# Gate logits and ranks of the second pass on four 128x32 column tiles each

## The chip, the cores and the metric

One core of a Trainium2 chip runs one program. The metric is the device time of one execution in microseconds (us); the median of three runs stands for a kernel. TensorE works on stationary weights (loaded by a weight load, LDWEIGHTS) and moving columns (MATMUL); an fp32 product is recorded as two pairs of load and matmul, a transpose as one pair.

## The reference

128 sequences of 32 tokens with 512 channels (4096 tokens) pass three residual layers: cross attention to a context, a gated delta-rule attention, and a mixture of eight experts of which each token takes two. What matters here is the end of the second layer and the third:

```python
ctx = _rmsnorm(ys, norm_w) * jax.nn.silu(gate)
x = x + (ctx.reshape(b, l, D_OUT) @ Wo.T + bo)
...
logits = xf @ gate_w.T                 # xf = layernorm(x), 4096 x 512; gate_w 8 x 512
w, sel = jax.lax.top_k(logits, TOP_K)  # two experts a token, softmax over the two
...
out = jnp.einsum('ne,ned->nd', w_full, expert_out)
```

## The kernel before

The tokens are cut into 32 units of 128 (NU = 32). A first pass computes cross attention, the projections and the delta rule and leaves its results in device memory; its loops are not touched. The second pass, which the function second_pass writes out without loops, has four parts:

- a stretch of turns w = 0 to 26 (BEFORE = 27), one after the other;
- the tiles of the first part of the tokens (24 units), each 128 rows for one expert (turn_tile, mix_tile);
- the remaining turns, w = 27 to 34, cut in three thirds each and placed between tiles 32 to 49 of that list (function inserted);
- the tiles of the second part, while GpSimd gathers the two results of each token and VectorE adds them up (combine).

A turn w is a pipeline stage that serves several units at once. TensorE does, in this order: (third 0) transposes the normalised rows x2n of unit w-3 into turn_bank, computes y of unit w+1 as 64 products of 32x32 tiles (make_y), transposes context of unit w-1; (third 1) the logits of unit w-3 from x2n_t and gate, then the output product wo of unit w-1; (third 2) the ranks of unit w-3, which count how many earlier tokens chose each expert. The logits have the stationary operand x2n_t (four chunks of 128x128) and eight moving columns; the ranks have two stationary 128x128 matrices (earlier, ones) and eight moving columns. Both go through the helper products at L118 to L121, as does wo, so that all three carry line L120 in the profile; they are told apart by the names of their tiles (small_bank<-gate,x2n_t; small_bank<-member,earlier; small_bank<-taken,ones; wo_bank<-wo,context_t).

Between the two transposes ScalarE copies turn_bank out (move_x2n L1410, move_context L1404): the logits wait for the first copy, wo for the second. VectorE takes the logits in choose (L1503 to L1518), which ends with the tile taken; the ranks wait for that (member_ready). VectorE then uses the ranks in place (L1527), which gives each token its row for the scatter that GpSimd issues. A turn's x2n for the next transposes comes from VectorE as well (scaled, L1497). Each engine runs its own list in order and waits on semaphores. SyncE issues the loads and stores of each unit, the experts' weights (1 MB each, in every second turn at first) and the tiles' rows.

Of the kernel before, what the change touches and what calls it, by code (L numbers as in the profile page):

```python
# [12 lines left out]
B, N, D = 128, 32, 512  # L13
M, C = 257, 384
H, HD = 16, 32
E = 8
P = 128
BU = P // N
NU = B // BU
DC, CC = D // P, C // P  # L20
# [97 lines left out]
def products(pe, out, terms, start=True, stop=True):  # L118
    for i, (lhs_t, rhs) in enumerate(terms):
        last = pe.matmul(out, lhs_t, rhs, start=start and i == 0, stop=stop and i == len(terms) - 1)  # L120
    return last  # L121
# [971 lines left out]
def second_pass(nc, ident, early, rows, wo_t, bo, gate_t, expert_t, out):  # L1093
    with ExitStack() as ctx:
        def sb(name, shape, dt=F32):
            return ctx.enter_context(nc.sbuf_tensor(name, shape, dt))

        def sem(name):
            return ctx.enter_context(nc.semaphore(name))
# [6 lines left out]
        gate = sb("gate", [P, DC, E])  # L1106
        bo_s = sb("bo_s", [P, D])
        earlier = sb("earlier", [P, P])
        ones = sb("ones", [P, P])
# [19 lines left out]
        x2n_t = sb("x2n_t", [P, DC, P])  # L1129
# [12 lines left out]
        member = sb("member", [P, 2, E])  # L1142
        taken = sb("taken", [P, 2, E])
# [23 lines left out]
        small_bank = ctx.enter_context(nc.psum_tensor("small_bank", [P, D], F32))  # L1167
# [17 lines left out]
        member_ready, ranks_ready, ranks_read = sem("member_ready"), sem("ranks_ready"), sem("ranks_read")  # L1185
# [24 lines left out]
        def inserted(t):  # L1210

            n, places = 3 * (NU + 3 - BEFORE), INSERT_END - INSERT_AT
            return [(BEFORE + i // 3, i % 3) for i in range(n) if INSERT_AT + i * places // n == t]
# [383 lines left out]
        @block.tensor  # L1597
        def _(pe):
            def make_y(w):
                g, q = w // GU, w % GU  # L1600
                if q == 0 or w == 0:
                    pe.wait_ge(group_loaded[g % 2], (g // 2) * 320 + 320)
                if w > 1:
                    pe.wait_ge(y_read, w - 1)
                for h in range(H):
                    for b in range(BU):
                        seq, at, head = slice(N * q, N * q + N), slice(N * b, N * b + N), slice(HD * h, HD * h + HD)
                        last = pe.matmul(y[at, w % 2, head], qk[g % 2][seq, b, head], delta[g % 2][seq, b, head],  # L1608
                                         start=True, stop=True)
                last.then_inc(y_ready, 1)  # L1610

            def turn_rows(to, row, done):
                for c in range(DC):
                    last = pe.transpose(to[:, c, :], row[:, c * P:c * P + P], ident[:])  # L1614
                last.then_inc(done, 1)

            def turn(w, third):
                if third == 0:
                    if w >= 3:
                        pe.wait_ge(x2n_ready, w - 2)  # L1620
                        pe.wait_ge(context_moved, min(w - 1, NU))
                        turn_rows(turn_bank, x2n[:, (w - 3) % 2], x2n_turned)
                    if w + 1 < NU:
                        make_y(w + 1)
                    if 0 <= w - 1 < NU:
                        pe.wait_ge(context_ready, w)
                        if w > 2:
                            pe.wait_ge(x2n_moved, w - 2)
                        turn_rows(turn_bank, context[:, (w - 1) % 2], context_turned)
                if third == 1:  # L1630
                    if w >= 3:
                        pe.wait_ge(x2n_moved, w - 2)
                        if w > 3:
                            pe.wait_ge(ranks_read, w - 3)
                        products(pe, small_bank[:, 0:E], [(x2n_t[:, c, :], gate[:, c, :]) for c in range(DC)])\
                            .then_inc(logits_ready, 1)
                    if 0 <= w - 1 < NU:
                        pe.wait_ge(context_moved, w)
                        if w > 1:
                            pe.wait_ge(x2_ready, w - 1)  # L1640
                        products(pe, wo_bank[:], [(context_t[:, c, :], wo[:, c, :]) for c in range(DC)])\
                            .then_inc(wo_ready, 1)
                if third == 2 and w >= 3:
                    r = w - 3
                    pe.wait_ge(member_ready, r + 1)
                    products(pe, small_bank[:, E:2 * E],
                             [(earlier[:], member[:, r % 2]), (ones[:], taken[:, r % 2])]).then_inc(ranks_ready, 1)
                    if r + 1 in (FIRST[1], NU):
                        pe.matmul(small_bank[:, 2 * E:3 * E], ones[:], taken[:, (r + 1) % 2], start=True, stop=True)\
                            .then_inc(totals_ready, 1)  # L1650

            def turn_tile(t):
                pe.wait_ge(xs_loaded[t % 4], 16 * (t // 4) + 16)
                if t > 0:
                    pe.wait_ge(xs_moved, t)
                turn_rows(xs_bank, xs[:, t % 4], xs_turned)

            def mix_tile(t, expert):
                pe.wait_ge(xs_moved, t + 1)
                if t >= 2:  # L1660
                    pe.wait_ge(y_moved, t - 1)
                products(pe, mix[t % 2][:], [(xs_t[:, t % 2, c, :], experts[:, bass.ds(expert + c * D, D)])
                                             for c in range(DC)]).then_inc(mixed, 1)

            def expert_of(t):
                part = int(t >= START[1])
                if t in START:
                    pe.wait_ge(lists_ready, part + 1)
                return pe.value_load(expert_at[0:1, part, t - START[part]:t - START[part] + 1], min_val=0,
                                     max_val=(E - 1) * DC * D)  # L1670

            make_y(0)
            for w in range(BEFORE):
                for third in range(3):
                    if (w, third) == (1, 1):
                        pe.wait_ge(outputs_loaded, 32)
                    if (w, third) == (3, 2):
                        pe.wait_ge(constants, 1)
                    turn(w, third)
            pe.wait_ge(experts_loaded, 16 * E)  # L1680
            expert = expert_of(0)
            turn_tile(0)
            for t in range(sum(TILES)):
                if t + 1 < sum(TILES):
                    following = expert_of(t + 1)
                    turn_tile(t + 1)
                mix_tile(t, expert)
                expert = following
                for w, third in inserted(t):
                    turn(w, third)  # L1690
# [43 lines left out]
```

## Time and profile before

| | |
|---|---|
| median of three runs | 3275.37 us (3274.96 to 3275.93) |
| span of the profiled execution | 3280.0 us |
| first pass, to about | 2590 us |
| turns w = 3 to 26 | 2622.82 to 2847.65 us |
| turns between tiles | 2990 to 3125 us |

The profiled execution's own time is its span, from the first to the last instruction; no further time of it is given, and it lies 4.6 us above the median. In the profile, PE is TensorE's matmul side and PEld its weight loads. A timeline line gives the start in us, the duration, the engine, the kernel's line, the operation, output<-inputs, the shape of the tile (rows*columns of the array, then the moving operand), how many instructions are merged, and in brackets the idle time ahead and what ended it ("issue": nothing that the profile shows).

### The profile page before, as it was taken

What the parts mean: (1) busy time and instruction counts of PE and PEld (TensorE: products, weight loads), DVE (VectorE), ACT (ScalarE), POOL (GpSimd) and SP (SyncE); (2) the same over time, 40 slices, a digit from 0 to 9 for tenths busy, and PEclk for the clock granted to TensorE, in tenths of its full rate; (3) what the DMA queues carried; (4) which work ended last, traced back from release to release, by engine and by line L of the source; (5) the groups of instructions that cost most, each with busy time, mean ns of one, the idle gap of its engine ahead of it and who ended that gap; (6) DMA issues with size and microseconds to landing.
All of it is one profiled execution on the core that took longest, in us unless ns stands there. A gap on an engine that the chain in (4) does not pass through costs nothing. (4 is left out here: it accounts for less than half of the span.)

```text
span 3280.0 us, 87701 instructions
## 1 busy us (share of the span) xinstructions
PE 3097.4 (94%) x35570; PEld 2267.9 (69%) x35570; DVE 2009.3 (61%) x4107; ACT 1337.9 (41%) x3360; POOL 641.3 (20%) x514
## 2 busy tenths in 40 slices
PE   7999999999999999999999999999999788898984
PEld 5777777777777777777777777777777455544542
DVE  3333367666776677666667766667676477893323
ACT  3444444444444444444444444444443233322321
POOL 0011111111111111111111111111111376601234
PEclk9999999999999999999999999999999888899997
DMA  4222322232222222322232223222321688545479
GB/s 168 69 73 76 105 93 91 86 103 84 81 79 98 85 81 85 98 84 81 79 102 90 81 79 102 84 81 86 108 82 55 170 255 247 166 135 157 145 264 324
DMA packets 297853, 378.10 MB, mean 115 GB/s; under 512 B 159568, under 2 KB 211536, under 8 KB 296016
## 3 DMA queue, kind: packets, MB, share of 16 engines
q1 hardware_dynamic: 287184, 338.19, 32.7%
q0 software_dynamic: 10240, 33.56, 3.0%
q8 instruction: 346, 5.67, 0.7%
q14 instruction: 83, 0.68, 0.1%
HBM read 258.17 MB, written 189.01 MB: 136 GB/s over the span
## 5 line engine op out<-in xcount | busy, mean ns | idle before, releaser
L120 PE MATMUL ring<-cond_high,wkv_high 128*128 128x342 f32 (+1 forms) x1152 | 404.6, 351 | 43.7 <-issue 20.8
L120 PE MATMUL ring<-cond_low,wkv_high 128*128 128x342 f32 (+1 forms) x1152 | 371.4, 322 | 0.0
L120 PE MATMUL ring<-cond_high,wkv_low 128*128 128x342 f32 (+1 forms) x1152 | 370.3, 321 | 0.0
L615 ACT ACTIVATE shared_rows<-ring,kvb 128x342 f32<-128x342 f32 (+1 forms) x384 | 209.6, 546 | 376.6 <-PE ring L120 376.6
L840 DVE TENSOR_REDUCE neg_max<-score 128x4 f32<-128x1028 f32 x128 | 157.3, 1229 | 288.3 <-PE score L952 288.3
L120 PE MATMUL ring<-wkv_high,cond_high 128*128 128x512 f32 x768 | 316.6, 412 | 0.0
L169 DVE TENSOR_TENSOR prod<-coef,deltas 128x64 f32<-128x64 f32 (+30 forms) x248 | 306.8, 1237 | 5.9
L120 PE MATMUL ring<-wkv_high,cond_low 128*128 128x512 f32 x768 | 303.1, 395 | 0.0
L120 PE MATMUL ring<-wkv_low,cond_high 128*128 128x512 f32 x768 | 302.7, 394 | 0.0
L649 ACT ACTIVATE prob<-score,neg_max 128x257 f32<-128x257 f32 x512 | 236.5, 475 | 135.3 <-DVE neg_max L840 135.3
L120 PE MATMUL mix<-experts,xs_t 128*128 x624 | 287.1, 604 | 0.0
L120 PEld LDWEIGHTS ring<-cond_high,wkv_high 128*128 128x128 f32 x1152 | 219.0, 190 | 92.9 <-issue 54.2
L173 DVE TENSOR_TENSOR prod<-prod 128x256 f32<-128x256 f32 (+5 forms) x352 | 258.1, 733 | 12.1
L569 POOL TENSOR_TENSOR vgb<-vgb,steps_of 128x512 f32<-128x512 f32 x32 | 40.5, 1265 | 1067.2 <-ACT steps_of L644 1067.2
L120 PE MATMUL ring<-wattn,x1n_t 128*128 128x512 f32 x512 | 246.7, 615 | 0.3 <-ACT prob L622 0.3
L120 PE MATMUL ring<-x1n_t,wattn 128*128 128x128 f32 x2048 | 238.9, 278 | 0.0
L120 PEld LDWEIGHTS ring<-x1n_t,wattn 128*128 128x128 f32 x2048 | 233.7, 194 | 0.0
L120 PEld LDWEIGHTS ring<-cond_low,wkv_high 128*128 128x128 f32 x1152 | 218.6, 190 | 15.1 <-issue 15.1
L610 ACT ACTIVATE v_s<-ring 128x512 f32<-128x512 f32 x256 | 154.4, 603 | 157.8 <-PE ring L120 157.8
L120 PEld LDWEIGHTS ring<-cond_high,wkv_low 128*128 128x128 f32 x1152 | 218.7, 190 | 0.0
L120 PEld LDWEIGHTS mix<-experts,xs_t 128*128 128x128 f32 x624 | 115.3, 195 | 116.5 <-issue 116.5
L120 PEld LDWEIGHTS ring<-wkv_high,cond_high 128*128 128x128 f32 x768 | 144.4, 188 | 63.1 <-issue 34.8
(199 smaller groups left out, 5499.8 us busy)
## 6 DMA issues: line engine op xcount, KB each, us to landing
cond<-cond_t_dram SPq DMA_DIRECT2D x128, 385.5 KB, 4.2
xs<-slot_rows SPq DMA_DIRECT2D x78, 256.0 KB, 2.8
slot_rows<-ys SPq DMA_DIRECT2D x78, 256.0 KB, 2.0
x_rows<-x SPq DMA_DIRECT2D x64, 256.0 KB, 2.7
vb_rows<-vgb SPq DMA_DIRECT2D x64, 256.0 KB, 3.4
x_in<-x_dram SPq DMA_DIRECT2D x32, 256.0 KB, 3.4
kk_rows<-kk_rows_s SPq DMA_DIRECT2D x32, 256.0 KB, 2.7
qk_rows<-decay SPq DMA_DIRECT2D x32, 256.0 KB, 2.8
```

What stands on the lines that cost most here:

```text
L120: last = pe.matmul(out, lhs_t, rhs, start=start and i == 0, stop=stop and i == len(terms) - 1)
L169: own.then(dve.tensor_tensor(tiles["prod"][:, 0:t], coef, tiles["deltas"][:, 0:t], ALU.mult))
L173: own.then(dve.tensor_tensor(tiles["prod"][:, 0:half], tiles["prod"][:, 0:half], tiles["prod"][:, left:whole], ALU.add))
L569: own.then(pool.tensor_tensor(vgb[:, 1], vgb[:, 1], steps_of[:].rearrange("p h t -> p (h t)"), ALU.mult))
L610: act.activation(dst, ring_bank[bank][:], func, **how).then_inc(ring.free[bank], 1)
L615: act.activation(k_t[:, group, at:at + n], ring_bank[bank][:, 0:n], ACT.Identity, bias=kvb[:, group:group + 1]).then_inc(ring.free[bank], 1)
L649: act.activation(prob[:, b % 2, g, :], score[:, g, 0:M], ACT.Exp, bias=neg_max[:, g:g + 1], accum_out=sums[:, g:g + 1]).then_inc(exp_done, 1)
L840: dve.tensor_reduce(neg_max[:], score[:, :, 0:M], AX.X, ALU.max, negate=True)\
```

## The change

The products of the logits and of the ranks no longer go through products but through a new by_quarter, which cuts the stationary operand into four blocks of 32 columns. Each block gives 32 of the 128 output partitions, in its own 128x32 column tile of the array. One product becomes four. The operands, the waits, the semaphores and the order of the work stay as they are; the single product for the totals stays whole.

```diff
+            def by_quarter(out, terms):
+                for i, (lhs_t, rhs) in enumerate(terms):
+                    for at in range(0, P, N):
+                        last = pe.matmul(out[at:at + N, :], lhs_t[:, at:at + N], rhs, start=(i == 0),
+                                         stop=(i == len(terms) - 1))
+                return last
+
...
-                        products(pe, small_bank[:, 0:E], [(x2n_t[:, c, :], gate[:, c, :]) for c in range(DC)])\
+                        by_quarter(small_bank[:, 0:E], [(x2n_t[:, c, :], gate[:, c, :]) for c in range(DC)])\
                             .then_inc(logits_ready, 1)
...
-                    products(pe, small_bank[:, E:2 * E],
-                             [(earlier[:], member[:, r % 2]), (ones[:], taken[:, r % 2])]).then_inc(ranks_ready, 1)
+                    by_quarter(small_bank[:, E:2 * E],
+                               [(earlier[:], member[:, r % 2]), (ones[:], taken[:, r % 2])]).then_inc(ranks_ready, 1)
```

N is 32, P is 128.

## Rows read from the trace of the kernel before

**Rows 1.** The page's first line.
```profile
span 3280.0 us, 87701 instructions
```

**Rows 2.** Windows: stretch and its us, busy us (instructions) by engine, PEclk, DMA share, GB/s.
```profile
2622.82:2847.65 224.83, 200.41 (x3746) 132.00 (x3746) 177.59 (x573) 80.58 (x168) 159.55 (x118) 0.86 0.81 233
...
2990.00:3125.00 135.00, 126.05 (x964) 71.50 (x965) 44.78 (x180) 46.88 (x92) 35.91 (x30) 0.96 0.45 150
```

**Rows 3.** Windows of two turns, and of 20 turns in a row.
```profile
2707.39:2714.42 7.03, 7.03 (x159) 4.91 (x158) 6.27 (x25) 3.31 (x7) 4.50 (x3) 1.00 0.45 121
...
2722.29:2730.87 8.58, 7.72 (x156) 5.05 (x156) 7.88 (x25) 3.44 (x8) 6.74 (x6) 1.00 1.12 318
2629.87:2820.13 190.26, 167.25 (x3122) 110.15 (x3122) 148.14 (x482) 67.01 (x140) 133.02 (x98) 0.86 0.87 248
```

**Rows 4.** Timeline of TensorE's matmuls in the shortest of these turns.
```profile
2707.96 1.29 PE L1608 MATMUL y<-delta,qk 32*32 32x32 f32 x128
2709.17 0.66 PE L1614 MATMUL turn_bank<-ident,context 128*128 128x128 f32 x4
2709.66 0.96 PE L120 MATMUL small_bank<-gate,x2n_t 128*128 128x8 f32 x8
2710.52 3.70 PE L120 MATMUL wo_bank<-wo,context_t 128*128 128x512 f32 x8
2714.05 0.28 PE L120 MATMUL small_bank<-member,earlier 128*128 128x8 f32 x2
...
2714.42 0.63 PE L1614 MATMUL turn_bank<-ident,x2n 128*128 128x128 f32 x4
```

**Rows 5.** The same view at the ranks two turns later.
```profile
2729.99 0.39 PE L120 MATMUL small_bank<-member,earlier 128*128 128x8 f32 x2 [0.51 <-DVE taken L1518]
```

**Rows 6.** Windows of six turns: two of them, and the sum line of all six.
```profile
2645.35:2656.97 11.62, 10.00 (x156) 6.52 (x157) 8.62 (x26) 4.87 (x11) 9.44 (x8) 0.71 1.09 299
...
2682.32:2691.53 9.21, 9.12 (x157) 5.68 (x157) 8.52 (x26) 4.33 (x9) 7.27 (x6) 0.81 0.95 263
...
sum 79.35, PE 61.31 PEld 39.29 DVE 49.39 ACT 22.74 POOL 50.54; mean PE 10.22 PEld 6.55 DVE 8.23 ACT 3.79 POOL 8.42
```

**Rows 7.** Timeline of TensorE's matmuls in three of these turns.
```profile
2645.93 1.67 PE L1608 MATMUL y<-delta,qk 32*32 32x32 f32 x128
...
2649.86 1.45 PE L120 MATMUL small_bank<-gate,x2n_t 128*128 128x8 f32 x6 [1.54 <-issue]
...
2657.53 1.09 PE L1608 MATMUL y<-shared_rows 32*32 32x32 f32 x104
2660.17 0.39 PE L1608 MATMUL y<-shared_rows 32*32 32x32 f32 x24 [1.55 <-issue]
...
2697.98 0.44 PE L1608 MATMUL y<-delta,qk 32*32 32x32 f32 x16 [4.73 <-issue]
```

**Rows 8.** DMA view, 2622 to 2848: queue, packets, MB, share of 16 engines.
```profile
q8 instruction: 29, 0.48, 0.9%
```

**Rows 9.** Timeline of TensorE's matmuls in the first pass, around a column-tiled group.
```profile
1503.76 0.39 PE L120 MATMUL ring<-wkv_low,cond_high 128*128 128x512 f32 x1
1503.99 0.40 PE L120 MATMUL ring<-wkv_high,cond_low 128*128 128x512 f32 x1
1504.31 0.76 PE L982 MATMUL ring<-prob_t,v_s 128*32 128x32 f32 x64
1505.01 0.42 PE L986 MATMUL ring<-prob_last_t,v_last_s 4*32 4x128 f32 x8
```

**Rows 10.** Timeline of all engines in the turn of rows 4.
```profile
2709.86 0.60 ACT L1404 ACTIVATE context_t<-turn_bank 128x512 f32<-128x512 f32 x1 [1.21 <-PE turn_bank L1614]
...
2710.51 0.30 PEld L120 LDWEIGHTS wo_bank<-wo,context_t 128*128 128x128 f32 x2
```

**Rows 11.** Timeline of TensorE's matmuls between tiles.
```profile
3038.70 0.95 PE L120 MATMUL small_bank<-gate,x2n_t 128*128 128x8 f32 x8
3039.51 3.68 PE L120 MATMUL wo_bank<-wo,context_t 128*128 128x512 f32 x8
```

## The prediction

> **What bounds the kernel now.** I read the page first: the profiled execution spans 3280.0 us [rows 1], 4.6 us over the median of the timed runs (3275.37). I make the sum against the span and carry the difference over to the median unchanged. The changed lines run only in the second pass, so I split that pass by windows [rows 2]. Two stretches hold them: 2622.82 to 2847.65 (stage A: 24 turns of the second pass back to back, w = 3 to 26, 224.83 us, granted clock 0.86 on the mean, DMA share 0.81) and 2990 to 3125 (stage B: the last 8 turns between expert tiles, TensorE busy 126.05 of 135 us). Whatever stage A gains or loses moves all that follows, since the expert tiles start only after the last ranks of stage A.
>
> In stage A the reader is to look at single turns. The shortest takes 7.03 us [rows 3], and in it TensorE has no gap [rows 4]: y, the turned context, logits (2709.66 to 2710.52, 0.86 us), wo (3.53 us), ranks (0.37 us), the turned x2n. The turn but one after it takes 8.58 us at the full clock [rows 3], and ends in a wait of TensorE, 0.51 us, for VectorE's taken [rows 5]. So TensorE and VectorE are almost equally long per turn. But the mean of 20 turns is 190.26 / 20 = 9.5 us [rows 3]: 49.7 us above 20 x 7.03. Most of that lies in six turns, together 79.35 us, or 37.2 above 6 x 7.03 [rows 6]. Each holds a gap of TensorE marked "issue" (three of them in [rows 7]): between two matmuls of one group, with no semaphore in between. After such a gap the granted clock is at its lower level (1.2 GHz) for part of the turn (on the mean 0.81 even in the cheapest of the six [rows 6]).
>
> **What these gaps are.** Count the matmuls from the gap at 2649.86 to the gap at 2660.17: 6 logits, 8 wo, 4 ranks, 4 turns of x2n, 104 of y [rows 4, 7] make 126. Each has its weight load: 252 instructions, with three or four waits 256. The DMA view gives 29 instruction packets of 16 KB for stage A [rows 8], and 2 x 3746 matmuls and loads [rows 2] with four waits a turn, over 256, are 29.6. So TensorE takes its instructions in blocks of 256 by DMA, and a gap is a block that came late, with the data queues at 0.81 of the DMA engines. In the turn from 2645.35 two block ends lie close together, one 14 instructions into y, which starts at 2645.93, the other after two of the eight logits matmuls [rows 7]: the next block was there only at 2649.86, 3.9 us after the first end.
>
> The Trainium skill, Runtime: NRT & Kernel Launch, section Instruction fetch mechanics, also has 16 KiB blocks of 256 instructions, fetched while the current one runs, but holds the cost of a block's end to be mostly hidden. The gaps of stage A speak against the second half; by the rule the sum would be that of rival 1.
>
> **The change part by part.** *Logits.* Eight pairs of load and matmul become 32, each load of 32 columns. The trace has this form in the first pass: 64 pairs of 128x32 tiles from 1504.31 to 1505.01, 0.70 us or 11 ns a pair [rows 9]; the 128 pairs of y take 1.21 us or 9.5 ns [rows 4]. So 32 pairs take 0.30 to 0.35 us. Going into the tiled form costs 0.09 us: the 512-column matmul before it holds TensorE 0.32 us (1503.99 to 1504.31) where the one ahead of it held TensorE 0.23 us (1503.76 to 1503.99). Coming back, wo's first load can no longer run ahead; no row isolates that, so between nothing and two pairs of loads (2 x 0.107 us, from 0.86 / 8); I take one. Together 0.09 + 0.35 + 0.11 = 0.55 us (0.39 to 0.65) against 0.86: 0.3 us less.
>
> *Is that on the path?* In stage A, no: ScalarE copies the turned context from 2709.86 to 2710.46, and wo's first load goes at 2710.51 [rows 10]. It waits for that copy, which the logits just cover; shorter logits leave TensorE idle in its place. Uncovered, 0.3 us a turn would be 7 us. Where the clock is low the logits outlast the copy, so I credit 0.3 us in stalled turns. In stage B, six turns of eight have a tile between the turned context and the logits, so the copy is long done and wo follows at once (3038.70 to 3039.51 [rows 11]): 6 x 0.27 = 1.6 us less.
>
> *Ranks.* Four pairs in 0.37 us become 16: 0.09 + 16 x 0.011 + 0.11 = 0.38 us. Nothing, within 0.1 us either way (8 turns of B: 0.8 us at most; in A taken by the slack towards VectorE).
>
> *Instructions.* Logits +48, ranks +24: a turn grows from 312 and four waits (316) to 388. Blocks per turn go from 1.23 to 1.52; two turns are 776 = 3 x 256 + 8, so block ends recur at the same places every second turn, 8 earlier each time. Where? Before, a turn moves them 60 earlier. From instruction 270 of the fourth turn (the gap at 2649.86) back over three turns: 194 into the y of the first turn, and nothing ahead of it changes. From there on, at 388 a turn: ends at 62 and 318 in the second turn, 54 and 310 in the fourth, down to 6 and 262 in the sixteenth, -2 and 254, -10 and 246 after that. y covers 0 to 255, the logits 268 to 332. So in some ten turns a whole block lies in y and logits, which TensorE eats in some 1.2 + 0.5 + 0.2 = 1.9 us; the trace showed 3.9 us for its delivery. Before, such a pair of ends came about every fifth turn.
>
> The sum over the same 20 turns. Of the ten stalled ones I price each as the turn from 2645.35, whose block ends lie alike: 11.62 us [rows 6], 4.6 over 7.03. Of the other 20 blocks I let three be late by chance, as two of about 20 were before, at the mean of six turns, 37.2 / 6 = 6.2 us. That is 46 + 18.6 = 64.6; less 0.3 x 13 = 4 for the logits; plus 3 for VectorE's waits in the seven quiet turns (up to 1.55 us a turn before, as 8.58 shows; less now, since each stall lets VectorE catch up). 63.6 against 49.7: **14 us more**. Bounds: at the cheapest stall (9.21 - 7.03 = 2.2 us [rows 6]) it is 39.6, 10 us less than before; at 6.2 us each it is 80, 30 more. I take the middle one because its geometry is the new one. Stage B: -1.6, and 1 for one late block in its eight turns. Sum +13.4: span 3293, median **3289 us**.
>
> **The rivals.** *1. Blocks arrive in time or their lateness is lost in VectorE's lag.* Then stage B's 1.6 us and some 0.4 us in six half-clock turns are all: -4, **3271**. For it: after 2813 the gaps are gone, and longer turns thin out the DMA traffic. Against: 3.9 us for a block that is eaten in 1.9. It decides once a block is there in 2 us.
>
> *2. Faster: the logits are on the path.* If wo could start when they end, 24 x 0.3 + 1.6 = 9 us go: **3266**. For it: TensorE has no gap in the shortest turn. Against: wo's load at 2710.51, 0.05 us behind the copy's end. It decides where ScalarE's copy ends before the logits do. The Trainium skill, TensorEngine Tiling (Array Packing), section Theoretical Speedup, allows up to 4x for 32-wide tiles; by that the logits would take an estimated 0.21 us, and 0.65 x 24 + 3.6 make 19 us.
>
> *3. The changes of form cost more than 0.09 us.* Four a turn stand where none stood. From 0.25 us each at both ends the logits gain nothing (0.25 + 0.35 + 0.25) and the ranks lose 0.3 us in each of 32 turns (0.25 + 0.18 + 0.25 against 0.37): 10 us, **3285** without any late block. Against: the two rows that show such a change.
>
> **How the numbers follow.** Forecast 0.62, rival 1 0.17, rival 2 0.11, rival 3 0.10. A measurement of this kernel tells 0.2% (6.5 us) from no change. The forecast's own range is 3277 to 3306 and gives 0.56 to slower and 0.06 to same; rival 1 gives 0.14 to same and 0.03 to faster; rival 2 0.11 to faster; rival 3 0.08 to slower and 0.02 to same. Faster 0.14, same 0.22, slower 0.64. The range is 3269 to 3306: below lies rival 2 and the tail of rival 1, above a mean stall beyond 6.2 us.
>
> **What would show it.** Right: logits at 0.5 us in quiet turns while wo still starts 0.05 us behind ScalarE's copy; 35 to 37 instruction packets in stage A; "issue" gaps in y, the turned context or the logits of every second turn from the second on; a lower mean clock in stage A; logits and wo 0.3 us closer in stage B. Wrong: gaps as many as before or all under 1 us; wo following the logits directly; or logits still at 0.8 us.

## The result and the profile after

The changed kernel takes 3288.85 us against 3277.6 us (medians of 20 runs each, side by side on one chip), a ratio of 1.0031 with an interval of 1.002 to 1.0042: slower by 0.31%, some 10 us. The forecast was 3289 us and slower. The runs of one kernel scatter more than the first three showed (3271.66 to 3291.59 before, 3278.96 to 3301.98 after), and single profiles scatter likewise, which the readings below have to bear. The profiled execution took 3290.16 us; its page begins

```profile
span 3288.1 us, 90005 instructions
```

Its span is 8.1 us above that of before [rows 1]. Windows of the kernel after (stretch and its us, busy us and instructions by engine, granted clock, DMA share, GB/s), as in [rows 2, 3]:

```profile
2622.70:2853.90 231.20, 188.27 (x4609) 108.43 (x4610) 175.32 (x573) 80.26 (x168) 157.46 (x116) 0.86 0.76 225
...
2629.74:2828.70 198.96, 159.34 (x3847) 91.42 (x3841) 147.91 (x482) 66.95 (x140) 133.56 (x98) 0.85 0.81 238
2702.34:2709.36 7.02, 6.70 (x202) 4.02 (x193) 6.27 (x25) 3.31 (x7) 4.50 (x3) 1.00 0.46 125
2709.36:2722.78 13.42, 9.13 (x202) 5.05 (x193) 9.47 (x25) 3.42 (x7) 8.96 (x7) 0.75 0.88 274
```

The reader is to see three things. Stage A takes 231.2 us, 6.6 more than between the same two instructions before (224.6, to 2847.4), and the 20 turns of [rows 3] take 198.96 instead of 190.26: 8.7 more, of which the other four turns, one ahead of them and three behind, give 2.1 back (32.2 us, before 34.3). A quiet turn is as long as ever, 7.02 us, although TensorE is now busy for only 6.70 of it. And every second turn looks like the last line: 13.42 us, at a granted clock of 0.75. In it TensorE stands still for 4.29 us in the logits, and wo behind them runs at the lower clock: 5.87 us, where a quiet turn's wo takes 3.70.

```profile
2716.73 5.87 PE L120 MATMUL wo_bank<-wo,context_t 128*128 128x512 f32 x8
```

The DMA view of stage A, queue of the instructions, as in [rows 8]: 36 packets where 29 were, 0.59 MB, which is 16.4 KB each.

```profile
q8 instruction: 36, 0.59, 1.1%
```

The timeline of TensorE's matmuls, the counterpart of [rows 7]: the first seven of the stage's 11 gaps over 1 us (five were there before), and one in the turned context and one in y, from later turns. After "x" stands how many matmuls of the group were still to come.

```profile
2635.12 0.24 PE L1620 MATMUL small_bank<-gate,x2n_t 128*32 128x8 f32 x6 [2.57 <-issue]
...
2652.86 0.38 PE L1620 MATMUL small_bank<-gate,x2n_t 128*32 128x8 f32 x10 [2.23 <-issue]
...
2673.93 0.40 PE L1620 MATMUL small_bank<-gate,x2n_t 128*32 128x8 f32 x15 [5.14 <-issue]
...
2695.92 0.50 PE L1620 MATMUL small_bank<-gate,x2n_t 128*32 128x8 f32 x19 [5.15 <-issue]
...
2716.29 0.51 PE L1620 MATMUL small_bank<-gate,x2n_t 128*32 128x8 f32 x23 [4.29 <-issue]
...
2735.19 0.60 PE L1620 MATMUL small_bank<-gate,x2n_t 128*32 128x8 f32 x27 [2.78 <-issue]
...
2756.45 0.62 PE L1620 MATMUL small_bank<-gate,x2n_t 128*32 128x8 f32 x32 [4.47 <-issue]
...
2776.90 0.90 PE L1614 MATMUL turn_bank<-ident,context 128*128 128x128 f32 x3 [4.36 <-issue]
...
2795.28 0.25 PE L1608 MATMUL y<-delta,qk 32*32 32x32 f32 x3 [2.05 <-issue]
```

The gaps move forward by four or five pairs from one to the next, that is by 8 to 10 instructions every second turn, through the logits, then the turned context, then y: a period of 256 instructions against two turns of 776. All 11 lie in every second turn.

The trace's list of DMA packets has the blocks themselves. Ahead of each of the 11 gaps' ends a 16 KB packet of the instruction queue moves for 0.89 to 1.22 us and lands 1.30 to 1.54 us before the matmuls go on; ahead of the five gaps of before it lands 1.26 to 1.47 us before. In the five gaps of over 4 us the packet starts to move only 1.9 to 2.9 us after the gap has begun. So a gap is a late block, and what is late is the start of its transfer.

All engines in the quiet turn, as in [rows 4, 10]:

```profile
2704.14 0.66 PE L1614 MATMUL turn_bank<-ident,context 128*128 128x128 f32 x4
...
2704.73 0.44 PE L1620 MATMUL small_bank<-gate,x2n_t 128*32 128x8 f32 x32
2704.84 0.60 ACT L1404 ACTIVATE context_t<-turn_bank 128x512 f32<-128x512 f32 x1 [1.21 <-PE turn_bank L1614]
...
2705.49 0.30 PEld L120 LDWEIGHTS wo_bank<-wo,context_t 128*128 128x128 f32 x2 [0.41 <-ACT context_t L1404]
```

The logits take 0.44 us instead of 0.96 by this view. The load for wo comes at 2705.49, 0.05 us behind the end of ScalarE's copy (2704.84 + 0.60), as before; what the logits saved has become a wait of 0.41 us.

Stage B, from the x2n transposes of w = 27 to the last ranks, by windows. Before:

```profile
3001.84:3114.50 112.66, 109.83 (x919) 63.19 (x918) 41.28 (x163) 42.60 (x85) 33.99 (x28) 1.00 0.42 144
```

After:

```profile
3009.84:3124.84 115.00, 108.33 (x1207) 56.15 (x1205) 41.29 (x163) 42.56 (x85) 33.98 (x28) 1.00 0.42 141
```

TensorE is busy 1.5 us less and the stage is 2.34 us longer; 0.6 less was forecast. The timeline of TensorE's matmuls after shows where; its logits are to be set beside those of [rows 11]:

```profile
3032.13 0.44 PE L1620 MATMUL small_bank<-gate,x2n_t 128*32 128x8 f32 x32
3032.49 3.70 PE L120 MATMUL wo_bank<-wo,context_t 128*128 128x512 f32 x8
3036.12 0.25 PE L1620 MATMUL small_bank<-member,earlier 128*32 128x8 f32 x8
3036.21 0.23 PE L1620 MATMUL small_bank<-taken,ones 128*32 128x8 f32 x8
...
3036.90 0.63 PE L1614 MATMUL xs_bank<-ident,xs 128*128 128x128 f32 x4 [0.46 <-issue]
```

And before, the same ranks and the tile's transposes behind them:

```profile
3027.69 0.28 PE L120 MATMUL small_bank<-member,earlier 128*128 128x8 f32 x2
3027.83 0.37 PE L120 MATMUL small_bank<-taken,ones 128*128 128x8 f32 x2
3028.06 0.63 PE L1614 MATMUL xs_bank<-ident,xs 128*128 128x128 f32 x4
```

From the logits to wo 0.36 us pass where 0.81 did. But from the ranks to the next tile 0.78 us pass (3036.12 to 3036.90) where 0.37 did, and 0.46 of them are "issue". Six of the eight rank groups are followed by a tile and take 0.77 to 0.82 us; the two that are followed by x2n transposes take 0.24, less than before. In the last two turns a tile follows the logits, and there 0.86 and 1.12 us pass up to it, so that the logits gain 1.6 us over the stage (6.56 to 4.97) and not 8 x 0.45.

### The profile page after: what moved, and what is told of

Read it like the earlier page. It is cut to its first block and busy times, and to the rows that moved or that the text cites. A ratio compares the mean times of both kernels' runs of the same rounds, so it can differ in the third digit from the quotient of the medians.

```text
span 3288.1 us, 90005 instructions
## 1 busy us (share of the span) xinstructions
PE 3081.9 (94%) x36722; PEld 2235.9 (68%) x36722; DVE 2008.4 (61%) x4107; ACT 1337.4 (41%) x3360; POOL 638.5 (19%) x514
## 5 line engine op out<-in xcount | busy, mean ns | idle before, releaser
L120 PE MATMUL ring<-wattn,x1n_t 128*128 128x512 f32 x512 | 246.7, 615 | 0.3 <-ACT prob L622 0.3
```

## The experiments

All kernels of one group of chip runs were timed beside the kernel before on the same chip; that kernel's medians were 3274.71, 3282.53 and 3282.85 us in the three groups (3277.6 beside the kernel after), so only ratios are compared. "Per turn" counts TensorE's instructions in a turn of stage A with its four waits. Stage times are those of one profile each.

| kernel | per turn | ratio of times | stage A, us | stage B, us |
|---|---|---|---|---|
| before | 316 | | 224.6 | 112.7 |
| after | 388 | 1.0031 [1.002, 1.0042] | 231.2 | 115.0 |
| logits alone | 364 | 1.0011 [0.9998, 1.0024] | 223.7 | 112.4 |
| ranks alone | 340 | 0.999 [0.9975, 1.0004] | 223.3 | 115.8 |
| y repeats, no tiles | 388 | 1.0088 [1.0066, 1.0109] | 246.7 | |
| one y repeat, no tiles | 320 | 0.9983 [0.9972, 0.9995] | 222.7 | 112.5 |
| block ends in wo | 384 | 1.0014 [0.9998, 1.0029] | 229.9 | 111.4 |
| block ends in logits | 384 | 1.0048 [1.0029, 1.0067] | 247.5 | |
| tiles late | 320 | 1.0005 [0.9987, 1.0023] | 214.8 | 118.4 |
| experts' loads first | 388 | one run | 224.8 | |
| expert read early | 388 | 1.001 [0.9995, 1.0026] | 227.1 | 109.0 |
| logits late | 320 | 0.9972 [0.9953, 0.999] | 216.2 | 111.3 |
| tiles late, read early | 320 | 0.9985 [0.997, 0.9999] | 214.9 | 110.5 |

### Each half alone

Logits on column tiles, ranks as before:

```diff
-                    by_quarter(small_bank[:, E:2 * E],
-                               [(earlier[:], member[:, r % 2]), (ones[:], taken[:, r % 2])]).then_inc(ranks_ready, 1)
+                    products(pe, small_bank[:, E:2 * E],
+                             [(earlier[:], member[:, r % 2]), (ones[:], taken[:, r % 2])]).then_inc(ranks_ready, 1)
```

> The logits on column tiles, the ranks whole. Theory (late instruction blocks): a turn has 364 instructions instead of 316, block ends move 108 a turn, and a whole block lies in y, turned context and logits (or from the ranks to the next y) in about 8 of 24 turns, against 5 before and 11 after: 5 us over before (0 to 9), some 8 instruction gaps of over 1 us in stage A. Rival A (the change of form is what costs): two changes of form a turn instead of four, 5 us over before too, but with as few gaps as before. Rival B (the logits' saving reaches the path): faster than before.

Measured: 1.0011, not to be told from no change, with ten gaps over 1 us in stage A (27.3 us together, 15.8 before) but a stage no longer than before. So more gaps do not by themselves make a longer stage: before, turns without a gap take up to 8.58 us [rows 3] with TensorE waiting for VectorE, and behind a stalled turn such waits are missing (7.02 us after). In stage B the logits fall to 5.00 us in all (6.56 before) and the ranks stay at 3.13.

Ranks on column tiles, logits as before:

```diff
-                        by_quarter(small_bank[:, 0:E], [(x2n_t[:, c, :], gate[:, c, :]) for c in range(DC)])\
+                        products(pe, small_bank[:, 0:E], [(x2n_t[:, c, :], gate[:, c, :]) for c in range(DC)])\
```

> The ranks on column tiles, the logits whole. Theory: 340 instructions a turn, block ends move 84 a turn, a short block every third turn, of which only some four end before wo: 1 us over before (-3 to 4), 4 to 6 gaps of over 1 us. Rival A: 5 us over before, as with the logits alone.

Measured: 0.999, five gaps, stage B 115.8 us. The ranks take 5.19 us in stage B instead of 3.13, with the whole logits beside them: the loss of stage B is theirs alone, and it is there with or without the tiled logits.

### Instructions without tiles

The same number of instructions as after, by computing some y products twice in the turns of stage A, in the kernel before:

```diff
-                for h in range(H):
-                    for b in range(BU):
...
+                pairs = [(h, b) for h in range(H) for b in range(BU)]
+                more = 18 if 3 < w <= BEFORE else 0
+                for h, b in pairs + pairs[len(pairs) - more:]:
...
```

> The kernel before, with no new column tile: 18 of y's 64 products of each unit from the turn w = 3 on are computed a second time, with the same operands into the same place. That adds 72 instructions a turn, as many as the change, in the form that y has anyway. Theory: 388 instructions a turn, so block ends stand as after the change and TensorE waits in every second turn; 11 us as after, plus 0.3 us for the repeats in the quiet turns: 14 us over before (8 to 20), some 11 gaps. Rival A: no new change of form, so only the repeats' 0.3 us in the turns that TensorE sets: 2 to 4 us over before, with five or six gaps.

Measured: 1.0088, 29 us, with gaps in every second turn again, nine of them over 1 us. The timeline of TensorE's matmuls of this kernel:

```profile
2630.54 0.32 PE L1609 MATMUL y<-delta,qk 32*32 32x32 f32 x5 [2.53 <-issue]
...
2653.88 0.36 PE L1609 MATMUL y<-delta,qk 32*32 32x32 f32 x9 [5.53 <-issue]
...
2677.05 0.43 PE L1609 MATMUL y<-shared_rows 32*32 32x32 f32 x14 [5.10 <-issue]
```

Column tiles are not needed for the gaps: 72 more cheap instructions a turn make them by themselves, and again the gap moves by four or five pairs each time. The size was missed by half, the loss being twice the 14 us forecast. Part of it is the repeats' own time: a quiet turn takes 7.35 us instead of 7.02, some 8 us over 24 turns of the 22 that stage A is longer than before. The gaps over 1 us are not longer (32.0 us together, 37.6 after), but stalled turns take 10 to 16 us here. One reason that fits is that these gaps lie in y, ahead of the turned context and so ahead of ScalarE's copy, where those of the change mostly lie in the logits, beside it; that is argued and no run separates it.

One repeated product a turn (and six once), so that the turn has 320 instructions, 5/4 of a block:

```diff
+                more = 1 if 3 < w <= BEFORE else 6 if w == 3 else 0
```

> The kernel before, with one of y's products repeated in each turn from w = 3 on (4 instructions, 320 a turn) and six repeated once in the turn ahead (24 instructions). Four turns are then five blocks exactly, and the one turn in four that has two block ends has the second in the middle of wo, so that no block is eaten in under 3.8 us. Theory: gaps are left only where a block waits over 2 us longer than usual behind data: 2 to 4 of them, 5 us under before (-12 to 0). Rivals: 20 to 40 ns a turn more, no difference that can be measured, five or six gaps.

Measured: 0.9983, about 5.6 us faster with work added, nearly what was expected. But five gaps exceed 1 us (1.06 to 3.55), so the block ends were not all freed; the time came as expected, its picture only in part.

### Where the block ends lie

Two kernels with tiled logits, whole ranks and five repeats a turn (384 instructions, 3/2 of a block, so that ends stay where they are put): the first with 22 repeats once at the start, which puts one of the three block ends of two turns into wo and the others into y, the second with 5, which leaves one in the logits.

```diff
+                more = 5 if 3 < w <= BEFORE else 22 if w == 3 else 0
```

> The logits on column tiles, the ranks whole, five of y's products repeated in each turn from w = 3 on: 384 instructions a turn, so two turns are three blocks and the block ends stay where they are. 22 products repeated once in the turn ahead put the ends at about 102 and 230 of y and in the middle of wo. Theory: no block is eaten in under 3.6 us, so only a block that waits long behind data comes late: 3 to 5 gaps of over 1 us, and the time at or below that of before (-8 to +2). Rival A (the forms cost): within 3 us of the next kernel.

```diff
+                more = 5 if 3 < w <= BEFORE else 5 if w == 3 else 0
```

> The same kernel with 5 instead of 22 products repeated once: 68 instructions less in the whole program, 384 a turn as well. The ends now lie at about 42 and 170 of y and in the logits, so that in every second turn a block is eaten in about 1.7 us. Theory: 11 or 12 gaps in stage A, 12 to 25 us over the kernel with the ends in wo, although it does 0.3 us less work. Rival A: no difference, or 0.3 us faster.

Measured: 1.0014 and 1.0048. The second is some 10 us slower with 68 instructions fewer, so where the ends lie costs time by itself. But the first missed its expectation: eight gaps over 1 us remain in its matmuls (ten in its weight loads), where 3 to 5 were expected; the second has fourteen. Weight loads in its timeline:

```profile
2639.40 0.44 PEld L1609 LDWEIGHTS y<-delta,qk 32*32 32x32 f32 x21 [3.28 <-issue]
...
2654.62 0.19 PEld L120 LDWEIGHTS wo_bank<-wo,context_t 128*128 128x128 f32 x1 [1.46 <-issue]
...
2662.85 0.50 PEld L1609 LDWEIGHTS y<-delta,qk 32*32 32x32 f32 x21 [4.94 <-issue]
```

The block that came at 2654.62, with wo's last three matmuls, was eaten by 2657.91 (2662.85 - 4.94). That is 3.3 us instead of the 1.9 that the prediction set against a delivery of 3.9, and the next one still came 4.94 us late, 8.2 us after the block ahead of it. So in stage A not even a block of 3.3 us is safe. The timeline of TensorE's matmuls in the second kernel:

```profile
2652.63 0.51 PE L1621 MATMUL small_bank<-gate,x2n_t 128*32 128x8 f32 x24 [4.19 <-issue]
...
2673.92 0.51 PE L1621 MATMUL small_bank<-gate,x2n_t 128*32 128x8 f32 x25 [5.17 <-issue]
```

The gap in the logits stays at one place, as 3/2 of a block a turn says, and comes in every second turn.

### What makes a block late

The kernel after, with the experts' 8 MB loaded ahead of the second pass's first turn instead of between turns; DMA share in stage A falls from 0.76 to 0.70.

```diff
+            for e in range(E):
+                sp.dma_start(experts[:, e * DC * D:(e + 1) * DC * D].rearrange("p (c n) -> p c n", c=DC),
+                             expert_t[e].rearrange("(c p) n -> p c n", p=P)).then_inc(experts_loaded, 16)
             for w in range(BEFORE):
                 follow(w)
...
-                if w % 2 == 1 and w < 2 * E:
-                    e = w // 2
-                    sp.dma_start(experts[:, e * DC * D:(e + 1) * DC * D].rearrange("p (c n) -> p c n", c=DC),
-                                 expert_t[e].rearrange("(c p) n -> p c n", p=P)).then_inc(experts_loaded, 16)
```

> The changed kernel, with the loads of the experts' weights (8 x 1 MB) issued in one go ahead of turn 0 instead of one in every second turn up to w = 15. That leaves the instructions of TensorE as they are and takes 8 MB out of the queues during stage A. Theory: the gaps stay in every second turn at the same instructions, but those up to w = 16, 2.4 to 5.3 us in the changed kernel, shrink to 1.3 to 2.5 us, since a block no longer waits behind an expert; stage A gets shorter by 10 us or more, while the turns ahead of it start later. If the gaps were a cost of the forms, they would keep their lengths.

The timeline of its TensorE matmuls:

```profile
2655.66 0.29 PE L1619 MATMUL small_bank<-gate,x2n_t 128*32 128x8 f32 x6 [1.83 <-issue]
...
2673.26 0.38 PE L1619 MATMUL small_bank<-gate,x2n_t 128*32 128x8 f32 x10 [2.21 <-issue]
...
2691.97 0.31 PE L1619 MATMUL small_bank<-gate,x2n_t 128*32 128x8 f32 x15 [1.89 <-issue]
...
2709.49 0.36 PE L1619 MATMUL small_bank<-gate,x2n_t 128*32 128x8 f32 x19 [2.01 <-issue]
```

The same instructions as after (x6, x10, x15, x19) and shorter gaps: the first seven are 1.83, 2.21, 1.89, 2.01, 1.35, 2.98 and 1.21 us, 13.5 in all, where the kernel after has 26.6 and the kernel with the expert read early, whose stage A is the same, 22.3. In six of the seven the block's packet already moves when the gap begins. Stage A is 6.4 us shorter, less than the 10 or more expected, and no more than single profiles of one and the same stage A differ by (214.8 to 222.7 us with one repeat a turn). The whole kernel is not better (3301.74 us in its one timed run), because the loads hold up the start of stage A by 18 us (2640.92 instead of 2622.70). So the gaps depend on the traffic of the data queues, and some 2 us of each remain without the experts' loads.

### The tiles only where the path has use for them

Tiles in stage B alone (turns from w = 27 on), stage A with one repeat a turn as above; against the kernel after, cut:

```diff
-                        by_quarter(small_bank[:, 0:E], ...
+                        (by_quarter if w >= BEFORE else products)(pe, small_bank[:, 0:E], ...
-                    by_quarter(small_bank[:, E:2 * E], ...
+                    (by_quarter if w >= BEFORE else products)(pe, small_bank[:, E:2 * E], ...
```

> The column tiles only in the last eight turns, between the expert tiles, where wo follows the logits at once; in stage A both products whole, with one repeated product of y a turn (and six once) as in the kernel with 320 instructions a turn. Theory: 5 us under before as that kernel, and 0.35 us less in each of the six late turns that show the logits on the path, 2 us: 7 us under before (-13 to -2). If tiles cost in the late turns, it is no faster than the kernel with 320 instructions.

A miss: 1.0005. Stage A is short, 214.8 us, but stage B takes 118.4, even longer than after, with 5.24 us in the ranks. This, and the 0.46 us of "issue" after the ranks, brought up the suspicion that the next step tests. Ahead of each tile TensorE's program reads the tile's expert number into a register (expert_of). It may be that this read can't run ahead of 32 short rank instructions and stands in the open.

The kernel after, with that read moved ahead of the turn's inserted thirds:

```diff
             turn_tile(0)
+            following = expert_of(1)
             for t in range(sum(TILES)):
                 if t + 1 < sum(TILES):
-                    following = expert_of(t + 1)
                     turn_tile(t + 1)
                 mix_tile(t, expert)
                 expert = following
+                if t + 2 < sum(TILES):
+                    following = expert_of(t + 2)
                 for w, third in inserted(t):
                     turn(w, third)
```

> The changed kernel, in which TensorE reads the number of each tile's expert into a register (expert_of) one tile earlier: ahead of the inserted thirds of a turn instead of behind them. Theory: in the changed kernel the ranks' and logits' 96 instructions keep TensorE's sequencer from running ahead to that read, which costs 0.4 to 0.5 us behind the ranks in six of the last eight turns (0.77 to 0.82 us from ranks to the next tile, against 0.36 before). With the read ahead of them, behind a tile's 3.4 us, the ranks take 0.24 us in all eight turns and the stretch of these turns gets from 115.0 to 111 or 112 us (112.65 before); the total time 3 us under the changed kernel, still over before for stage A. Rival: the 0.4 us is a cost of going back from column tiles to transposes; then it stays.

The timeline of its TensorE matmuls at a tile after the ranks:

```profile
3030.89 0.25 PE L1620 MATMUL small_bank<-member,earlier 128*32 128x8 f32 x8
3030.97 0.23 PE L1620 MATMUL small_bank<-taken,ones 128*32 128x8 f32 x8
...
3031.13 0.66 PE L1614 MATMUL xs_bank<-ident,xs 128*128 128x128 f32 x4
```

and its windows:

```profile
2620.01:2847.07 227.06, 189.35 (x4609) 108.91 (x4610) 176.15 (x573) 80.48 (x168) 157.44 (x116) 0.86 0.79 229
3005.40:3114.40 109.00, 106.61 (x1207) 55.87 (x1206) 41.66 (x163) 42.34 (x85) 33.95 (x28) 1.00 0.44 149
```

The same 32 instructions now take 0.24 us up to the tile, 0.54 less than after and 0.13 less than the whole form. Stage B falls to 109.0 us, 6 below after and 3.7 below before, more than expected. So the loss behind the ranks was the read of the expert number, not the tiled form. The trace records the read itself: for the tile at 3028.06 before it ran from 3026.14 to 3026.44, under wo, and for the tile at 3036.90 after from 3036.15 to 3036.44, when the ranks had begun. But the 3.7 us below before are not all the tiles'. The read stood open in the kernel before too, behind the turned context:

```profile
3033.74 0.63 PE L1614 MATMUL turn_bank<-ident,context 128*128 128x128 f32 x4
3034.80 0.63 PE L1614 MATMUL xs_bank<-ident,xs 128*128 128x128 f32 x4 [0.43 <-issue]
```

From the turned context to the tile 0.75 to 1.06 us pass in four turns before, and 0.46 to 0.49 with the early read: 1.8 of the 3.7 us. The early read with both products whole was not run, so what the tiles are worth beside it is not shown. The whole kernel stands at 1.001, since stage A keeps ten of its gaps.

Tiled logits in stage B alone, whole ranks, one repeat a turn in stage A; against the kernel after, cut:

```diff
-                        by_quarter(small_bank[:, 0:E], ...
+                        (by_quarter if w >= BEFORE else products)(pe, small_bank[:, 0:E], ...
-                    by_quarter(small_bank[:, E:2 * E], ...
+                    products(pe, small_bank[:, E:2 * E], ...
```

> Column tiles for the logits of the last eight turns alone; ranks whole, stage A whole with 320 instructions a turn as in the kernel with one repeated product. Theory: stage A as in that kernel (6 us under before), the last eight turns 1.3 us shorter than before (111.4 us, as in the kernel with the block ends in wo): 7 us under before (-12 to -2), faster than both.

Measured: 0.9972, 9 us faster than before, the best of all; its interval lies wholly below 1, that of the kernel after wholly above. It overlaps that of the kernel with one repeat and no tiles (0.9983), so the timed runs do not show what the late tiles add. Its windows of the two stages:

```profile
2616.79:2833.02 216.23, 197.13 (x3793) 130.54 (x3794) 176.04 (x573) 80.23 (x168) 156.84 (x116) 0.88 0.82 241
2988.90:3100.20 111.30, 107.24 (x1110) 58.20 (x1108) 41.63 (x163) 42.39 (x85) 33.93 (x28) 1.00 0.43 146
```

In the profiles 1.4 us come from stage B, near the prediction's own term for the logits there (1.6). The rest comes from stage A, whose tensor work is that of the kernel before and one repeat.

Both tiled in stage B, with the early read and one repeat a turn in stage A:

> Both products on column tiles in the last eight turns alone, the expert's number read one tile earlier, stage A with 320 instructions a turn. Theory: the last eight turns at about 111 us (against 118.4 us in the kernel with late tiles and the late read, 112.65 before): 7 us under before (-12 to -2). If the ranks' 0.4 us stays, 4 us under before.

Measured: 0.9985, 5 us faster. Beside the same kernel without the early read (1.0005) that is 0.2%, where the two stages B differ by 7.9 us or 0.24%; the two intervals overlap. Of the 7.9, 1.57 us are a late block in the turned context of the kernel without it, whose packet lands 1.24 us before the matmuls go on.

## Why the prediction was right, and where it was not

**The late blocks: right, and shown.** The prediction's chain was more instructions, so more blocks, whose ends lie together in cheap work in every second turn. Packets were forecast at 35 to 37 and are 36. The gaps lie in every second turn from the second on, 8 to 10 instructions earlier each time. The kernel with y repeats shows that the count alone does it, the pair with ends put in wo and in the logits that the place counts, and the loads moved ahead that the data traffic sets the gaps' length. That an instruction packet lands 1.30 to 1.54 us before each gap's end shows directly that the gaps are late blocks. The Trainium skill, Runtime: NRT & Kernel Launch, section Instruction fetch mechanics, has blocks of 16 KiB or 256 instructions, and the 36 packets of 16.4 KB agree. It also holds the cost of a block's end to be mostly hidden; the gaps of 1.93 to 5.15 us disagree, and rival 1 with them.

**The size in stage A: right in sum by two errors.** Over the 20 turns the excess above 7.03 us a turn was forecast at 63.6 us and came to 58.4. The ten stalled turns were priced at 4.6 us each and cost 5.8 (128.3 us together, 58.0 above ten of 7.03). Of the 58.0, the gaps are 35.7 and wo at the lower clock 21.5: it takes 5.09 to 6.62 us in these turns and 3.70 in the quiet ones. The three further late blocks, 18.6 us, did not come, and the quiet turns' waits were priced at 3 us and cost 0.4. The price of 4.6 was read from one turn, and delivery turned out to take up to 8.2 us. The lower bound was misread: of the six turns of before that were said to hold a gap each, the cheapest (2682.32, 9.21 us) holds none over 0.1 us; its y takes 1.64 us and its wo 5.51 at the lower clock. The cheapest of the ten stalled turns after cost 3.65 us (10.68 - 7.03), not 2.2.

**The median: luck in part.** 3289 us was met to 0.2, but the sum forecast 13.4 us more than before, and the medians differ by 11.25, that of before having moved from 3275.37 to 3277.6. In the profiles the 20 turns gave 8.7 us where 14 were forecast, and stage B 2.34 more where 0.6 less was; the two misses partly cancel.

**The logits off the path in stage A: right, and shown.** Wo's load stands 0.05 us behind ScalarE's copy in both kernels, and the logits' 0.4 us have turned into TensorE's wait for it. Rival 2 is out. For the logits 0.55 us were estimated (0.39 to 0.65); the views give 0.44 as a span and 0.36 up to wo in stage B. There the 1.6 us forecast were met by two errors, six turns at 0.27 us each: only four turns have a tile between the turned context and the logits, and they gain 0.44; in two wo waits for ScalarE's copy, and they gain 0.09; in the last two the tile behind the logits waits for the expert read, and they lose 0.05 and 0.31. The Trainium skill, TensorEngine Tiling (Array Packing), section Theoretical Speedup, allows up to 4x; 0.81 to 0.36 us is 2.2x.

**The ranks: this step failed.** "Nothing, within 0.1 us either way (8 turns of B: 0.8 us at most)" looked at the products alone. They did get shorter, 0.24 us against 0.37, and the quiet turns of stage A did not get longer (7.02 us), so rival 3 is out as well. But their 32 instructions uncovered the register read behind them, 0.4 us in six of eight turns, and stage B became 2.34 us longer instead of 0.6 shorter. The early read shows it: without that, 0.24 us in all eight but the last.

**A lower mean clock in stage A: wrong.** It is 0.86 both times. Stalled turns run at 0.66 to 0.85, but the quiet ones between them at 1.00; before, the six turns of [rows 6] ran at 0.62 to 0.84.

**What stays open.** Four kernels with the same instructions in stage A (one repeat a turn) have stages of 214.8 to 222.7 us in their single profiles, and two with those of the kernel after 227.1 and 231.2. So the split of the 10 us into 6.6, 2.34 and the rest is good to several us only; the order of the two groups is clear, and before's 224.6 is a single draw. Y takes 0.8 us more in stage B after, in two turns, which was not followed up. And the early read was not tried on the kernel before.

## What to carry to other kernels

Count an engine's instructions beside its time: where a stretch is cut into many cheap ones, look whether its blocks of instructions are eaten faster than they are delivered under that stretch's DMA load, and where their ends lie. A shorter product is worth its saving only where the next instruction waits for it, so tile it where it does and leave it whole elsewhere: the logits' tiles in stage B alone, with a turn of 5/4 of a block, made 0.28% of gain out of 0.31% of loss, of which the turn's length alone shows 0.17%. And look for what ran ahead behind a slow instruction, a register read above all, before making it fast.

## What the runs showed of the hardware

Each of the 11 gaps of TensorE ended 1.30 to 1.54 us after a 16 KB packet of the instruction queue had landed. A block of 256 instructions came 8.2 us after the one ahead of it while the DMA engines were busy for 0.79 of the stage. A register read that ran 1.55 us ahead of four pairs of 128-column products in the turn shown, and cost nothing there, stood open with 0.4 us behind 16 pairs of 32 columns; read earlier, the wait was gone. And a product computed twice in each turn, four instructions more, made the kernel 0.17% faster (0.9972 to 0.9995).
